# Q's first block from exact codes, its cosine on GpSimd, and one buffer for O's codes, in a decoder layer on one core

## What is computed

```python
def _dequant(codes, scales):                    # codes 0..15, one scale per 128 rows and column
    w = codes.astype(jnp.float32) - 8.0
    return w * jnp.repeat(scales, 128, axis=0)

q = hidden_states @ _dequant(q_codes, q_scales)   # (1024, 32 heads * 128)
k = hidden_states @ _dequant(k_codes, k_scales)   # (1024, 8 heads * 128), v alike
...
q = _rope(q)
k = _rope(k)
...
scores = jnp.einsum('bhqd,bhkd->bhqk', q, k) * scale + mask[None, None]
attn = jax.nn.softmax(scores, axis=-1)
out = jnp.einsum('bhqk,bhkd->bhqd', attn, v)
out = out.transpose(0, 2, 1, 3).reshape(b, s, NH * HD)
return out @ _dequant(o_codes, o_scales)
...
x = x + _L0_attn_ref(_layernorm(x, axis=-1), ...)
x = x + _L0_xattn_ref(_layernorm(x, axis=-1), ctx_4096, ...)   # both operands rounded to 0..255
x = x + _L0_ffn_ref(_layernorm(x, axis=-1), L0_ffn_weight)     # weights made binary
```

## Time and profile before

| what | value |
|---|---|
| median of 3 runs | 1098.23 us (1096.35 to 1099.12) |
| profiled execution | 1096.75 us, span 1095.0 us |
| granted TensorE clock | 0.998 of full speed |
| context slots 8 to 39 | 388.0 us |
| weight slots 40 to 61 | 252.0 us |

### The profile page before, as it was taken

One profiled execution on the slowest core, in us unless ns is written; L12 is line 12 of the kernel. 1 busy time (PEld: TensorE's weight loads), 2 busy tenths in 40 slices (PEclk: granted clock), 3 DMA queues, 4 the chain that ended last, 5 costly groups with the idle time before them and its releaser, 6 DMA issues.

```text
span 1095.0 us, 18877 instructions
## 1 busy us (share of the span) xinstructions
PE 1050.8 (96%) x5416; PEld 507.9 (46%) x5416; DVE 930.0 (85%) x1738; ACT 692.5 (63%) x1499; POOL 721.3 (66%) x789
## 2 busy tenths in 40 slices
...
GB/s 340 205 162 147 97 73 40 166 146 158 154 161 135 156 155 159 137 154 161 151 139 155 161 148 132 153 158 156 149 157 167 143 134 118 108 117 57 99 98 84
DMA packets 309652, 155.74 MB, mean 142 GB/s; under 512 B 257712, under 2 KB 270256, under 8 KB 309584
## 3 DMA queue, kind: packets, MB, share of 16 engines
...
## 4 chain that ended last, share of the span: by engine, by line
PE 73%; DVE 9%; ACT 6%; POOL 5%; issue 3%; DMA 1%; ACTq 1%; SPq 1%; DVEq 0%; POOLq 0%
PE side_ps L721 9%; PE side_ps L893 9%; PE side_ps L723 9%; PE side_ps L722 9%; PE proj_ps L913 8%; PE out_ps L913 8%; PE proj_ps L1064 4%; PE score_ps L876 3%; PE score_ps L877 2%; PE score_ps L878 2%; PE proj_ps L1069 2%; PE score_ps L1035 2%; DVE stats L1755 1%; ACT prob L1240 1%; DVE x_acc L2022 1%
## 5 line engine op out<-in xcount | busy, mean ns | idle before, releaser
L1587 POOL TENSOR_TENSOR w_b<-prob,w_b 128x896 f16<-128x896 f32 (+2 forms) x192 | 189.0, 999 | 29.8 <-ACT w_b L1267 29.5
L721 PE MATMUL side_ps<-hT,w_a 128*128 128x512 f16 x504 | 191.1, 379 | 1.5 <-DVE rot L1942 1.5
L723 PE MATMUL side_ps<-hT,w_a 128*128 128x512 f16 x504 | 191.0, 379 | 0.0
L722 PE MATMUL side_ps<-hT,w_a 128*128 128x512 f16 x504 | 191.0, 379 | 0.0
L1580 POOL TENSOR_SCALAR prob<-prob,row_inv 128x512 f32<-128x512 f32 (+3 forms) x256 | 170.9, 682 | 23.3 <-DVE row_inv L2095 17.9
L2022 DVE SCALAR_TENSOR_TENSOR x_acc<-proj_ps,o_now,x_acc 128x1024 f32<-128x1024 f32 x120 | 153.5, 1279 | 38.3 <-PE proj_ps L913 38.3
L1240 ACT ACTIVATE prob<-score_ps,neg_max 128x512 f32<-128x512 f32 (+3 forms) x256 | 133.0, 522 | 47.3 <-DVE neg_max L1998 39.0
L1594 POOL TENSOR_TENSOR q_sb<-rot,q_sb 128x512 f16<-128x512 f32 x62 | 72.3, 1167 | 137.3 <-ACT q_sb L1230 137.3
L2022 DVE SCALAR_TENSOR_TENSOR x_acc<-out_ps,o_now,x_acc 128x1024 f32<-128x1024 f32 x120 | 152.6, 1272 | 0.0
L913 PE MATMUL out_ps<-work,w_b 128*128 128x512 f16 x496 | 127.3, 379 | 2.0 <-DVE x_acc L2022 2.0
L913 PE MATMUL proj_ps<-work,w_b 128*128 128x512 f16 x496 | 127.3, 379 | 1.9 <-DVE x_acc L2022 1.1
...
## 6 DMA issues: line engine op xcount, KB each, us to landing
stage_c<-in_codes_dram SPq DMA_DIRECT2D x72, 256.0 KB, 2.9
stage_o<-in_codes_dram SPq DMA_DIRECT2D x64, 256.0 KB, 3.9
stage_s<-in_scales_dram SPq DMA_DIRECT2D x64, 256.0 KB, 3.8
ctx_raw<-in_ctx_dram ACTq DMA_DIRECT2D x32, 256.0 KB, 3.3
...
k_sb<-in_codes_dram SPq DMA_DIRECT2D x16, 256.0 KB, 7.0
v_sb<-in_scales_dram SPq DMA_DIRECT2D x16, 256.0 KB, 7.2
```

What stands on the lines that cost most here:

```text
L721: pe.matmul(o, stat(0), mov(0), start=first, stop=False)
L722: pe.matmul(o, stat(0), mov(1), start=False, stop=False)
L723: return pe.matmul(o, stat(1), mov(0), start=False, stop=last)
L1587: ins = pool.tensor_tensor(prob16[:, 1, to:to + w], prob[:, at:at + w], prob16[:, 0, to:to + w], ALU.subtract)
```

## The change

From slot 4 on (`by_parts`) Q's projection is done in two parts. The first block of 128 rows is taken from the codes as they are (`q_exact`: two products, into `pv_ps`), ScalarE brings it to SBUF multiplied by its scales (`q_base`, into `q_sum_in`, the former second buffer of O's codes), blocks 1 to 7 go to `q_ps` with three products each, and VectorE adds the two (`q_join`). The swap then reads SBUF; the cosine is GpSimd's (`q_turn`, into `rot`), and `q_sum` adds `rot` and `swapped`, both in SBUF, behind all three maxima instead of between the first and the second. In every second slot the piece of Q's weights holds the exact block, so that the three cutting instructions leave out 128 of 512 columns and ScalarE has one more small one. `q_hi` moves behind the last exponential, `q_lo` behind the first two norms, `sine` to the start of GpSimd's slot, `ao_rest` to the next slot behind the first maximum, `piece_lo` behind the second `o_add`, `o_cut` ahead of `prob_split`. O's codes have one buffer, so its load waits for `o_cut` of the same slot. A table of Q's scales is loaded and made in the K stage, and `o_scales` copies one column more.

```diff
+            def q_exact(g, i):
+                ...
+                pe.wait_ge(piece_done, g * SLOTS + (2 * h + 2))
+                pe.wait_ge(ao_ready, p - 3)
+                for l in range(2):
+                    mm = pe.matmul(pv_ps, w_a[:, 0, ...], hT[:, l, 0, ...], start=l == 0, stop=l == 1)
+                mm.then_inc(q_exact_done, 1)
...
 q_part:
-                        pe.wait_ge(q_summed, p)
+                        pe.wait_ge(q_joined, p - FIRST_PIECES)
...
 weigh:
+                if not (known(p) and (p == 0 or p >= N_SLOTS - FIRST_PIECES + 1)):
+                    pe.wait_ge(q_based, p)
...
 TensorE's slot:
-                if has_ahead:
+                if has_ahead and parts:
+                    q_exact(*ahead)
+                elif has_ahead:
                     q_part(*ahead, range(0, 1))
+                if has_ahead and parts:
+                    q_part(*ahead, range(1, EARLY))
                 scores(p, i, g, 2)
                 if has_ahead:
-                    q_part(*ahead, range(1, 3))
+                    q_part(*ahead, range(EARLY if parts else 1, 3))
...
 ScalarE:
+            def q_base(g, i):
+                ...
+                act.wait_ge(q_exact_done, p - FIRST_PIECES + 1)
+                if not (known(p) and p == FIRST_PIECES):
+                    act.wait_ge(q_cosed, p)
+                ...
+                act.activation(q_sum_in, pv_ps, ACT.Copy, scale=o_now[:, (i // B + 1) % 2, CB:CB + 1])\
+                    .then_inc(q_based, 1)
...
-                swap(q_swap_of(p), q_bank(p), q_swapped)
+                if by_parts(p):
+                    act.wait_ge(q_joined, p - FIRST_PIECES + 1)
+                swap(q_swap_of(p), q_sum_in if by_parts(p) else q_bank(p), q_swapped)
...
 GpSimd:
+            def q_turn(p):
+                pool.wait_ge(q_joined, p - FIRST_PIECES + 1)
+                pool.wait_ge(q_ready, p)
+                pool.tensor_tensor(rot[:, :], q_sum_in, cos_t[:, :], ALU.mult).then_inc(q_cosed, 1)
...
+                    if not (known(p) and p >= N_SLOTS - 1) and by_parts(p + 1):
+                        sine(swapped[:, :], q_swapped, p + 1, q_sined)
+                        q_turn(p + 1)
...
 VectorE:
-                dve.tensor_tensor(q_rot(p), q_bank(p), q_swap_of(p), ALU.add).then_inc(q_summed, 1)
+                dve.tensor_tensor(q_rot(p), rot[:, :] if by_parts(p) else q_bank(p), q_swap_of(p), ALU.add)\
+                    .then_inc(q_summed, 1)
+
+            def q_join(p):
+                dve.wait_ge(q_done, p + 1)
+                dve.wait_ge(q_based, p - FIRST_PIECES + 1)
+                dve.tensor_tensor(q_sum_in, q_bank(p), q_sum_in, ALU.add).then_inc(q_joined, 1)
...
 scale_table:
+                dve.tensor_scalar(o_table[:, 0:NH - Q_LEAD, CB], rows[:, Q_LEAD:NH, 0], Q_UP, None, ALU.mult)
+                dve.tensor_scalar(o_table[:, NH - Q_LEAD:NH, CB], rows[:, NH - Q_LEAD:NH, 0], Q_UP, None, ALU.mult)
+                dve.tensor_scalar(o_now[:, 1, CB:CB + 1], rows[:, Q_LEAD - 1:Q_LEAD, 0], Q_UP, None, ALU.mult)\
+                    .then_inc(o_table_ready, 1)
...
 SyncE:
+            def next_o(g, i):
+                ...
+                sp.wait_ge(o_codes_done, p + 1)
+                load_o(o_index(*after), (i + 1) % 2)
```

More of the change, by code:

```diff
@@ L462, in build @@
         cc_ready = sem("cc_ready")
-        xs_landed = [sem(f"xs_landed{t}") for t in range(TT)]
         y_turned = sem("y_turned")
@@ L527, in known, with by_parts @@
             return isinstance(n, int)
+        def by_parts(p):
+            return not (known(p) and p < FIRST_PIECES)
         def each_group(eng, body):
@@ L676, in body @@
                         load_xs(1)
+                    if not (known(p) and p + 1 >= N_SLOTS):
+                        next_o(g, i)
                     turn(p)
@@ L1338, in slot @@
                 exps(p, i, 2)
+                if has_next and by_parts(p + 1):
+                    q_hi(p + 1)
                 if has_piece:
@@ L1344, in slot @@
                     wf_sign(wf_early(p))
+                o_cut(p, i)
                 prob_split(p, 0)
@@ L1691, in body @@
                     norm(2).then_inc(norm_done, 1)
+                    if not (known(p) and p >= N_SLOTS - 1) and by_parts(p + 1):
+                        q_lo(p + 1)
                     if with_ctx:
@@ L2053, in slot @@
                     maxima(p, i, 0)
+                    ao_rest(p - 2, i - 2)
                     o_add(p - 1, i - 1, 3)
@@ L2075, in slot @@
                     j = o_scales(g, i)
-                if i or known(p):
+                first = not (i or known(p))
+                if not first:
+                    maxima(p, i, 0)
+                if first:
+                    dve.wait_ge(q_ready, p + 1)
+                if has_prev and p_ge2:
+                    ao_rest(p - 2, (i - 2) % SLOTS)
+                if first:
                     maxima(p, i, 0)
@@ L2079, in slot @@
                     wf_difference(0)
-                if has_next:
+                if has_next and not by_parts(p + 1):
                     q_sum(p + 1)
-                if not (i or known(p)):
-                    maxima(p, i, 0)
                 if has_o and not (known(p) and p == O_LAG):
```

107 lines of the change are left out of this document (66 added, 41 removed).

## The result

The changed kernel takes 1106.76 us (median of 4 runs, 1105.20 to 1107.84) where the kernel before took 1098.01 in the same comparison. The ratio is 1.0082, with a 95% interval of 1.0067 to 1.0097: slower by 0.8%. The profiled execution took 1107.14 us, its span 1105.3.

What follows compares the result with a forecast made beforehand. TensorE was taken as the bound, within 0.25 and 0.12 us per slot. Terms of -12.0, +6.0, +1.2, -0.6, -0.6, -1.0, +1.8 and +0.5 summed to -4.7: 1092.05 us, plus 1.48 for the median, 1093.5 us; range 1080 to 1110.

Steps and rivals of the forecast that it cites:

- the lead of 1.0: Weight slots: TensorE notices the ring of waits only once its lead of about 1 us is gone, -1.0 us.
- TensorE's part: Slots with Q done by parts: one product of 55 goes, leaving 54 x 0.216 = 11.66 us per slot.
- Up to 0.1 us in odd slots: Odd slots: the first unit of O waits for ao_rest, ending at about 2.15 us, where that unit stands at 2.17.
- The ring in the weight slots: Weight slots: waits from q_join round to the next q_join take 11.58 us, with collisions 12.3 per slot; +6.0 us.
- The bounds of 11.75 and 12.7: Weight slots, ends of the 12.3 us forecast: only the first collision, or each waiting for nearly a whole instruction.
- The context slots: 32 context slots: 11.75 us each in place of 12.13, between 11.66 and 12.0; -12.0 us (-14.9 to -4).
- Context slots above 12: Profile after, q_lo to q_lo in the context slots: a sign that the prediction, 11.7 to 11.8 us, is wrong.
- The prediction's three terms: Odd slots, ahead of the first O unit: scores 0.65 us, a maximum and ao_rest some 0.6 each, ending at about 2.15.
- rival (c): Context slots gain the product alone, ao_rest replacing the waits that go: 11.91 us each, -6.9, so 1098.6 us; chance 0.10.
- The ends: K stage +0.5 us for the scale table; slots 60 and 61 -0.6; slot 62 and the last slot +1.8.
- (a): All slots: TensorE stays the bound everywhere, weight slots at 11.75 us, so 1077.8 us; chance 0.18.
- (b): Weight slots, VectorE from q_sum to q_join: collisions at their upper end, 12.7 us per slot, so 1112.9 us; chance 0.22.

Runs made afterwards that it cites:

- e1: The changed kernel with the copy o_scales moved behind the first maximum and ao_rest in odd slots: 1101.70 us, ratio 1.0038.
- e7: The changed kernel without waits that others imply on ScalarE and, for q_sum, on VectorE, so both loop bodies are shorter: 1095.11 us, ratio 0.9979.
- e14: The changed kernel with reached waits added in the K stage on ScalarE and VectorE, shifting the loop bodies at full length: 1099.27 us, ratio 1.0027.
- e8: The changed kernel with the copy o_scales later, sine and q_turn ahead of the second prob_rest, and implied waits left out: 1086.88 us, ratio 0.9904.
- e12: The kernel of e8 with ao_rest ahead of the first maximum in every slot on VectorE: 1101.11 us, ratio 1.0039.
- e10: The kernel of e8 with ao_part ahead of the two swaps on ScalarE: 1106.03 us, ratio 1.0090.
- e6: The changed kernel without waits on ScalarE that other waits imply, its loop body shorter: 1101.48 us, ratio 1.0034.
- e2: The changed kernel with sine and q_turn of the head after the next ahead of the second prob_rest on GpSimd: 1095.22 us, ratio 0.9980.
- e5: The changed kernel with the first maximum ahead of ao_rest on VectorE in each loop round's first slot too: 1106.33 us, ratio 1.0080.
- the three built on it: The kernel before with reached waits added in ScalarE's loop slot, VectorE's loop slot, or ScalarE's K stage: 1103.29, 1110.01 and 1101.31 us.

## Why the prediction was wrong

The forecast was 1093.5 us, the result 1106.8. Against the profiled execution it was -4.7 us where +10.3 of span came. By the stages of the ledger, in us:

| stage | forecast | measured |
|---|---|---|
| to slot 2 | +0.5 | -0.6 |
| slots 2 to 7 | +1.2 - 0.6 = +0.6 | +2.2 |
| context slots | -12.0 | +0.7 |
| slots 40 to 59 | +6.0, less the lead of 1.0 | +4.5 |
| slots 60 to 62 | -0.6 + 1.6 = +1.0 | +1.0 |
| from slot 63 on | +0.2 | +2.5 |

The step that failed is the one on the context slots, 12.7 of the 15.0 us between the two sums.

**TensorE's part** was right in its pace: 54 products, 11.66 us, and each even slot takes 11.68. Its sentence on the O unit was mis-sized. "Up to 0.1 us in odd slots" took the way over the maximum and `ao_rest` too short (below), and left out the copy `o_scales` ahead of the maximum. The copy of 128x8 had been harmless (ns min/median/max):

```profile
L2008 DVE COPY o_now<-work x32: 151/392/740, 210.9 to 937.5; 128x8 f32<-128x8 f32 x16, 128x8 f32 x16
```

After the change it is next to `prob_rest`, in slot 3 for nearly its whole length:

```profile
208.81 1.88 POOL L1642 TENSOR_TENSOR w_b<-prob,w_b 128x896 f16<-128x896 f32 x1 [0.66 <-ACT w_b L1319]
209.00 1.72 DVE L2089 COPY o_now<-work 128x9 f32<-128x9 f32 x1
...
210.63 0.69 DVE L2079 CUSTOM_DVE_ANT_0 score_ps<-score_ps,mask_b 128x512 f32<-128x512 f32 x1
...
211.24 0.68 DVE L2119 SCALAR_TENSOR_TENSOR work<-side_ps,work 128x512 f16<-128x512 f32 x1
...
212.02 1.87 PE L943 MATMUL proj_ps<-work,w_b 128*128 128x512 f16 x4 [2.49 <-issue]
```

The last row is TensorE after 2.49 us idle. Its four products took 1.87 us where the earlier trace rows has 1.03, since the granted clock was 0.68 over these 5 us (columns as in the earlier trace rows), a mix of 1.2 and 2.4 GHz:

```profile
210.00:215.00 5.00, 2.98 (x8) 1.09 (x9) 3.70 (x9) 2.92 (x10) 4.47 (x6) 0.68 0.70 158
```

With the copy later (e1) TensorE was idle for 1.93 us there, and they took 1.02 us. Of such a copy the Trainium skill, "SBUF — State Buffer", section "Who interferes with whom", says that it may take the port pair that GpSimd uses; the trace agrees: 31 of the 32 copies start within a `prob_rest` and end within 0.05 us of its end, and the one beside a norm takes 0.16 us.

**The ring in the weight slots** was right in its steps and its sum. VectorE, ScalarE and GpSimd after, one turn:

```profile
768.25 0.68 DVE L2015 TENSOR_TENSOR stage_o<-side_ps,stage_o 128x512 f32<-128x512 f32 x1
...
769.04 0.63 ACT L1185 ACTIVATE swapped<-stage_o 64x512 f32<-64x512 f32 x1 [1.18 <-DVE stage_o L2015]
...
770.33 0.60 ACT L1328 ACTIVATE work<-side_ps 128x512 f16<-128x512 f32 x1
...
771.51 1.06 POOL L1642 TENSOR_TENSOR w_b<-prob,w_b 128x128 f16<-128x128 f32 x2 [0.98 <-ACT w_b L1319]
...
773.21 1.27 POOL L1630 TENSOR_TENSOR swapped<-swapped,sin_t 128x512 f32<-128x512 f32 x1
...
774.43 1.27 POOL L1650 TENSOR_TENSOR rot<-stage_o,cos_t 128x512 f32<-128x512 f32 x1
...
775.80 0.82 DVE L2008 TENSOR_TENSOR rot<-rot,swapped 128x512 f32<-128x512 f32 x1 [0.53 <-issue]
776.54 0.16 DVE L2185 RECIPROCAL row_inv<-row_sum 128x3 f32<-128x3 f32 x1
...
779.24 1.01 DVE L1854 SCALAR_TENSOR_TENSOR w_a<-stage_s,w_a 128x512 f16<-128x512 f32 x1
780.17 0.59 DVE L2041 SCALAR_TENSOR_TENSOR w_b<-w_b,wf_mean 128x256 f32<-128x256 f32 x1
780.68 0.68 DVE L2015 TENSOR_TENSOR stage_o<-side_ps,stage_o 128x512 f32<-128x512 f32 x1
```

| step, start to start | forecast | measured |
|---|---|---|
| `q_join` to swap, two swaps, `ao_part` to `prob_rest` | 0.72, 1.27, 1.18 | 0.79, 1.29, 1.18 |
| to `sine`, `q_turn`, `q_sum` | 1.72, 1.23, 1.30 | 1.70, 1.22, 1.37 |
| `q_sum` with `wf_clip` beside it | 0.61 + 0.2 | 0.74 |
| reciprocal to `q_join`, with collisions | 3.55 + 0.5 | 4.14 |
| sum | 12.3 | 12.43, the next turn 12.17 |

20 slots cost 4.5 us, with 6.0 less 1.0 of lead forecast, and opening the ring brought 9.0 back. TensorE shows it from slot 44 on, once its lead is used up: even slots of 11.68 and odd ones of 12.92 us, 12.30 on average. The bounds of 11.75 and 12.7 were not reached.

**The context slots** were the step that failed: -12.0 us in the sum, +0.7 measured. "Context slots above 12", one of the signs named for being wrong, came true (12.13). Two terms hide in that. The first was missing: 7.8 us of instruction fetches at three turns of the loop, shown by e7 and e14. Nothing in the prediction looked at the instruction queue or asked where a loop body ends. The second was mis-sized: the first O unit's wait in odd slots, put at up to 0.1 us, is 0.35 to 0.39. Without the fetches (e7, e14) even slots take 11.68 us and odd ones 12.07, 11.90 on average (380.80 / 32) where the sum had 11.75, and this wait is the one gap between TensorE's products that is left in nearly all of them. An odd slot of e1, from its first score product on:

```profile
499.89 0.38 PE L904 MATMUL score_ps<-k_sb,q_sb 128*128 x1
...
500.85 0.70 DVE L2079 CUSTOM_DVE_ANT_0 score_ps<-score_ps,mask_b 128x512 f32<-128x512 f32 x1 [1.10 <-PE score_ps L906]
...
501.47 0.69 DVE L2119 SCALAR_TENSOR_TENSOR work<-side_ps,work 128x512 f16<-128x512 f32 x1
...
502.40 1.03 PE L943 MATMUL proj_ps<-work,w_b 128*128 128x512 f16 x4 [0.18 <-DVE work L2119]
```

The prediction's three terms, 0.65 and twice 0.6, add up to 1.85 us and were put at 2.15. Here the maximum starts at 0.96 us of the slot and not at 0.65, `ao_rest` ends at 2.27, and the O unit starts at 2.51, 0.24 behind that. In an even slot, where it waits for nothing, it starts at 2.17. The copy ahead of the maximum makes 0.39 of the 0.35. That is the mechanism of rival (c), `ao_rest` in place of the waits that go, and its 11.91 us. In e8 two things end at nearly the same time ahead of `ao_rest` in odd context slots, the maximum at 1.57 us of the slot and `ao_part` at 1.66 (medians). e12 took only the first out of the way and e10 only the second, so neither could bring the O unit forward by more than about 0.1 us.

**The ends.** To slot 2 it was -0.6 us where +0.5 was forecast. Slot 0 does start 0.4 us later, as forecast, but TensorE's wait for the exponentials in slot 1 is 1.0 us shorter, which the prediction does not have. Slots 2 to 7 cost 2.2 us in place of 0.6, 2.1 of them in slot 3. Slots 60 to 62 cost 1.0 as forecast, by two misses that cancel: slots 60 and 61 cost 0.2 in place of -0.6, slot 62 0.7 in place of 1.6. Behind slot 63 are 2.5 us more. Some 1.7 of these are TensorE's clock around the change of stage: the granted clock over 10 us was 0.83 before and 0.66 after (before, then after, columns as in the earlier trace rows).

```profile
975.00:985.00 10.00, 7.26 (x35) 3.59 (x36) 7.63 (x12) 7.41 (x10) 3.66 (x3) 0.83 0.01 2
```

```profile
985.00:995.00 10.00, 8.39 (x35) 4.09 (x36) 6.64 (x8) 6.26 (x9) 4.79 (x3) 0.66 0.00 0
```

Whether this belongs to the change is open. In e6, e7 and e10 it is 0.83, with 165.6 to 165.7 us from slot 63 on; in e2, e5 and e14 it is 0.66 again, with 167.1 to 168.0 us. The kernel before and the three built on it have 164.5 to 165.0 us.

**Rivals.** (a) fell. (b) was nearest in time, 1112.9 us, but not by its mechanism: its 12.7 us per weight slot did not come. (c) had the mechanism of the context slots and gave 1098.6; the 7.8 us of fetches are what it lacks most. The range of 1080 to 1110 held the time by luck: the part of it above 1101 was there for (b), and the time came by another way.
